# Maxima of score bounds in rounds of four banks, pieces of x through one bank, in a cross-attention kernel

## The chip, the cores and the metric

The kernel runs on one core of a Trainium2 chip. The time is the device time of one execution in microseconds (us), from the profiler's records of the core. A core has a matrix engine (TensorE, PE; its weight loads are listed apart, as PEld), a vector engine (VectorE, DVE), a scalar engine (ScalarE, ACT), GpSimd (POOL, hardly used here) and SyncE (SP), which here only issues DMAs. PE writes its results into PSUM, eight banks of 128 partitions x 512 floats, and DVE and ACT read them out.

## The reference

For each of four batches (x: 2048 rows of 640; context: 154 rows of 384, of which 150 are keys and 4 are extra tokens) it computes an ordinary attention of 8 heads over the 150 keys, and a second branch in which the four extra tokens make 384 query rows that attend over all 2048 rows of x, and whose result is projected and attends over four keys. Both are added, projected and added to x.

```python
query = hidden_states @ Wq
keyt, valt = enc @ Wk, enc @ Wv
hs = _mha(query, keyt, valt)                       # 8 heads, 150 keys
ca_q1 = jnp.einsum('btc,th->bch', ca, Wq_ca)       # 384 rows from 4 tokens
ca_q1 = ca_q1[:, indices, :]                       # rows repeated to 2048
ca_hs1 = _mha(ca_q1, residual, residual)           # attends over x itself
ca_q2 = ca_hs1 @ Wq
ca_hs2 = _mha(ca_q2, ca @ Wk_ca, ca @ Wv_ca)       # 4 keys
out = (hs + ca_hs2) @ Wout + b_out + residual
```

The softmax over 2048 rows needs, for each of the 384 rows and each head, the maximum of the scores. The kernel finds these maxima ahead of the exponentials, and that work is what the change concerns.

## The kernel before

Each batch runs through a sequence of stages, one after the other on every engine in an order written out by hand; the engines are tied together by semaphores. The stages of a batch are: keys and values; the *stage of products*; a stage of scores, exponentials and weighted sums of the second branch (`scores`, `weigh`); and sixteen tiles of 128 rows of the ordinary attention with the output projection. All batches do the same.

The stage of products works on x in four chunks (`i`) of 512 rows and five column tiles (`kt`) of 128, twenty *pieces*, numbered m = 5 i + kt; the text writes x0 to x19. For each piece PE transposes four squares into a PSUM bank (`turn_x`), ACT copies the bank to SBUF (`copy_x`, semaphore `xt_copied`), and PE multiplies the copy with a small matrix (`products`, four matmuls of 56 or 84 columns, listed as eight), which adds up over the five pieces of a chunk in two banks of `ps_w`. ACT then copies these sums to `y_all` (for chunk 0 DVE does one of the two banks), DVE splits a part of them into `gst` (`split_g`), PE transposes that into a piece bank (`turn_g`), and ACT copies it into `g` (`copy_g`, semaphore `g_ready`). Pieces of x and of g take their bank in turn: `piece_free` makes PE wait until the piece that used the bank has been copied.

A *unit of maxima* is one matmul of 12 or 28 rows by 512 columns (`max_unit`) for one chunk q, one third `ct` of the 384 rows and one of four groups `r`, which is a group of 32 rows of the array, and one read by DVE that takes the maximum over the 512 columns (`unit_maxima`, semaphore `max_free`). There are two phases of 48 units; phase 0 and twelve units of phase 1 (`UNITS_EARLY`) stand in the stage of products, in which `UNIT_ORDER` lists them, and `PHASE0_UNITS` is 60. The other 36 lie in the next stage. In the stage of products they go in triples (`TRIPLES` says behind which piece and which of three places), in the three banks of `ps_s`, which the matmuls of a triple fill next to each other in different row groups. A unit waits until the unit that had its bank before has been read. The first unit of a chunk waits for that chunk's g.

Between all that PE does matmuls of 128 x 512 for the first queries (`queries0`, 75 in a batch: five outputs j of 15 each), whose number behind each piece is `Q0_FILL`, ahead of the round and the products at the pieces in `Q0_ENDS`, behind them elsewhere; `Q0_SPLIT`, `Q0_TURNED` and `Q0_TRIPLE` are the numbers around the last g and between the last rounds. The first query of an output waits until DVE has taken the output before it from its bank. Behind the last round follow the remaining queries and `turn_ca(0)`, the three transposes of the maxima, on which the next stage rests.

What PE issues for one piece m is in this order: transposes of x(m); queries if m is in `Q0_ENDS`; triple at AFTER_TURNED; products(m - 1), with `turn_g` at every fifth; triple at AFTER_PRODUCTS; queries; triple at AFTER_QUERIES. DVE takes a chunk's twelve first units, then the split of the next g, then the chunk's other units, then the low part of the queries (`q0_lows`).

## Time and profile before

| | us |
|---|---|
| median of 3 timed runs | 1541.65 |
| lowest and highest | 1541.1, 1544.61 |
| the profiled execution's own time | 1540.79 |
| its span, first to last instruction | 1539.0 |
| TensorE busy in it | 1499.8 (97%) |
| VectorE busy | 791.1 (51%) |
| ScalarE busy | 620.0 (40%) |

The granted TensorE clock was 0.996 of full speed in the mean. Times in the rows are in microseconds from the span's start, unless marked ns. A matmul's row gives its full latency, and following ones overlap with it, so that the distance of starts is what an instruction costs PE. The line number of a matmul is that of a helper: L508 is any matmul, L518 any transpose; what tells them apart is the tile on the left of the arrow and the operands on its right. `ps_s<-ot,ca_mat` is a unit of maxima (`g` lies in the tile `ot`), `ps_w<-gyw_b,work` products, `ps_w<-xt_h,wq_h` and its like a query, `ps_t<-ident,xc` a piece of x, `ps_t<-ident,gst` a piece of g, `ps_s<-ident,cst` the transposes of the maxima.

### The profile page before, as it was taken

What the parts mean: (1) busy time and instruction counts of PE and PEld (TensorE: products, weight loads), DVE (VectorE), ACT (ScalarE), POOL (GpSimd) and SP (SyncE); (2) the same over time, 40 slices, a digit from 0 to 9 for tenths busy, and PEclk for the clock granted to TensorE, in tenths of its full rate; (3) what the DMA queues carried; (4) which work ended last, traced back from release to release, by engine and by line L of the source; (5) the groups of instructions that cost most, each with busy time, mean ns of one, the idle gap of its engine ahead of it and who ended that gap; (6) DMA issues with size and microseconds to landing.
All of it is one profiled execution on the core that took longest, in us unless ns stands there. A gap on an engine that the chain in (4) does not pass through costs nothing.

```text
span 1539.0 us, 24550 instructions
## 1 busy us (share of the span) xinstructions
PE 1499.8 (97%) x10306; PEld 1247.5 (81%) x10306; DVE 791.1 (51%) x1595; ACT 620.0 (40%) x1310; POOL 2.8 (0%) x12
## 2 busy tenths in 40 slices
PE   6999999999999999999999999999999999999998
PEld 4764699999976489999987549999998745999998
DVE  5686445344468453443447826335345882443533
ACT  1428723233243862332333584233333368333322
POOL 0000000000000000000000000000000000000000
PEclk9999999999999999999999999999999999999999
DMA  6530011130253001131035200204004510021101
GB/s 241 205 136 35 3 54 70 55 114 26 89 170 130 1 16 48 66 111 54 35 111 182 88 1 20 82 28 156 18 35 155 180 38 1 20 95 57 61 18 43
DMA packets 46680, 117.28 MB, mean 76 GB/s; under 512 B 3661, under 2 KB 5317, under 8 KB 45019
## 3 DMA queue, kind: packets, MB, share of 16 engines
q1 hardware_dynamic: 37036, 93.91, 17.4%
q10 hardware_dynamic: 9535, 21.80, 3.7%
q8 instruction: 82, 1.34, 0.3%
q14 instruction: 27, 0.22, 0.0%
HBM read 77.33 MB, written 39.17 MB: 76 GB/s over the span
## 4 chain that ended last, share of the span: by engine, by line
PE 91%; DVE 4%; ACT 2%; issue 2%; DMA 0%; SPq 0%
PE ps_w L508 46%; PE ps_s L508 19%; PE ps_t L508 16%; PE ps_t L518 5%; PE ps_w L518 3%; DVE unit_max L1311 2%; ACT work L1124 1%; PE ps_s L518 1%; ACT ot L1038 0%; DMA y_all<-in_L_xattn_Wv_ca_dram 0%; DVE ca_mat L1327 0%; DVE ot L1423 0%; ACT ot L1107 0%; DVE xt_l L1337 0%; ACT work L1021 0%
## 5 line engine op out<-in xcount | busy, mean ns | idle before, releaser
L508 PE MATMUL ps_w<-wo_h,ot 128*128 128x320 f32 x1280 | 310.4, 314 | 0.6 <-DVE ot L1423 0.6
L1311 DVE TENSOR_REDUCE unit_max<-ps_s 128x1 f32<-128x512 f32 x384 | 240.6, 683 | 53.1 <-PE ps_s L508 52.2
L1094 ACT ACTIVATE work<-ps_s,neg_max 128x150 f32<-128x150 f32 x512 | 152.5, 403 | 223.4 <-DVE neg_max L1369 223.4
L508 PEld LDWEIGHTS ps_w<-wo_h,ot 128*128 128x128 f32 x1280 | 220.3, 188 | 0.9 <-DVE ot L1423 0.9
L508 PE MATMUL ps_w<-wo_l,ot 128*128 128x320 f32 x640 | 197.4, 308 | 0.0
L508 PEld LDWEIGHTS ps_w<-v_all,work 120*128 120x128 f32 x1280 | 170.3, 190 | 3.0 <-issue 2.5
L508 PE MATMUL ps_w<-v_all,work 120*128 120x162 f32 (+1 forms) x1280 | 171.3, 288 | 0.0
L1365 DVE TENSOR_REDUCE neg_max<-ps_s 128x6 f32<-128x900 f32 x64 | 70.1, 1095 | 165.2 <-PE ps_s L508 165.2
L508 PE MATMUL ps_s<-keys_h,qt_h 128*128 128x300 f32 (+1 forms) x448 | 140.0, 313 | 0.0
L508 PE MATMUL ps_s<-keys_h,qt_l 128*128 128x300 f32 (+1 forms) x448 | 131.5, 294 | 0.0
L508 PE MATMUL ps_s<-keys_l,qt_h 128*128 128x300 f32 (+1 forms) x448 | 131.1, 293 | 0.0
L1434 DVE TENSOR_TENSOR work<-ps_w,xc 128x320 f32<-128x320 f32 x128 | 62.4, 488 | 130.9 <-PE ps_w L508 130.9
L1391 DVE TENSOR_TENSOR qt_l<-ps_t,qt_h 128x512 fp32r<-128x512 f32 x60 | 41.5, 691 | 162.1 <-ACT qt_h L1076 162.1
L508 PEld LDWEIGHTS ps_w<-wo_l,ot 128*128 128x128 f32 x640 | 120.4, 188 | 0.2
L508 PE MATMUL ps_t<-xt_h,wq_h 128*128 128x512 f32 x300 | 119.3, 398 | 0.4
L1124 ACT ACTIVATE work<-ps_w 128x768 f32<-128x768 f32 x128 | 104.2, 814 | 35.2 <-PE ps_t L508 20.8
L508 PE MATMUL ps_t<-xt_h,wq_l 128*128 128x512 f32 x300 | 117.7, 392 | 0.0
L508 PE MATMUL ps_t<-xt_l,wq_h 128*128 128x512 f32 x300 | 116.6, 389 | 0.0
L1107 ACT ACTIVATE ot<-ps_w 128x640 fp32r<-128x640 f32 x64 | 45.0, 704 | 175.1 <-PE ps_w L518 175.1
L508 PE MATMUL ps_w<-work,y_all 128*32 128x384 f32 x1024 | 109.1, 498 | 0.1
L508 PEld LDWEIGHTS ps_s<-keys_h,qt_h 128*128 128x128 f32 x448 | 84.9, 189 | 25.5 <-issue 25.0
L1076 ACT ACTIVATE qt_h<-ps_t 128x512 fp32r<-128x512 f32 x60 | 35.9, 598 | 169.3 <-PE ps_t L508 169.3
(163 smaller groups left out, 2346.9 us busy)
## 6 DMA issues: line engine op xcount, KB each, us to landing
xc<-in_x_dram SPq DMA_DIRECT2D x32, 1280.0 KB, 6.5
out_dram<-work ACTq DMA_DIRECT2D x64, 320.0 KB, 2.2
xt_all<-work SPq DMA_DIRECT2D x60, 256.0 KB, 2.2
xt_l<-xt_all SPq DMA_DIRECT2D x12, 1280.0 KB, 5.6
y_all<-in_L_xattn_Wk_dram SPq DMA_DIRECT2D x4, 960.0 KB
y_all<-in_L_xattn_Wv_dram SPq DMA_DIRECT2D x4, 960.0 KB
pick<-pick_all SPq DMA_DIRECT2D x16, 194.0 KB
xc<-in_L_xattn_Wq_dram SPq DMA_DIRECT2D x1, 1600.0 KB, 10.5
```

Source lines behind the costliest of these rows:

```text
L508: return nc.tensor.matmul(out, lhs, rhs, start=start, stop=stop, skip_group_check=True)
L518: return nc.tensor.transpose(out, in_, ident[0:k, 0:k])
L1076: nc.scalar.activation(dst, ps_t[:, bank_of(use), :], copy).then_inc(t_high, 1)
L1094: return nc.scalar.activation(probs[:, h * KEYS:(h + 1) * KEYS], ps_s[:, bank, c * KEYS:(c + 1) * KEYS], exp, bias=neg_max[:, s % 2, h:h + ...
L1107: nc.scalar.activation(ot_h[:, s % 2, :], ot_psum, copy).then_inc(ot_high, 1)
L1124: nc.scalar.activation(e_buf[n % E_BUFS][:, 2 * p:2 * p + 2, :], score_banks[p], exp, scale=SCALE).then_inc(w_ready, 1)
L1311: v.tensor_reduce(unit_max[:, a, n, q:q + 1], bank, AX_X, ALU.max).then_inc(max_free, 1)
L1365: v.tensor_reduce(neg_max[:, s % 2, 0:6].rearrange("p (a h) -> p a h", a=2), ps_s[:, 0:2, 0:3 * KEYS].rearrange("p a (h k) -> p a h k", h= ...
L1391: v.tensor_tensor(dst, ps_t[:, bank_of(use), :], high_part, ALU.subtract).then_inc(t_free[bank_of(use)], 1)
L1434: v.tensor_tensor(o_tile[:, s % 2, cols], out_banks[half], xc[:, c % 2 * ST + t, cols], ALU.add).then_inc((ya_ready, y_ready)[half], 1)
```

## The change

Units of the stage of products go in rounds of four (`G_BANKS`), one in each row group, in the three banks of `ps_s` and in bank 1 of `ps_t`. Behind them three banks are used as before. `UNIT_BANK` and `UNIT_PREVIOUS` say which bank a unit has and which unit had it before. Pieces of x and of g all take bank 0 of `ps_t`; `piece_free` waits for the copy of the piece just ahead, where it waited for the one before that. Chunk 0 has eight early units of phase 1 and chunk 1 four (six and six before), so that each chunk is made of whole rounds. `TRIPLES` becomes `ROUNDS`, at most one round at a piece, and there is none at piece 16; `Q0_FILL` and `Q0_ENDS` have other numbers, and all remaining queries stand behind the last round, ahead of `turn_ca`.

```diff
--- before.py
+++ after.py
@@ -121,12 +121,12 @@
 SW = GYW + 1
 PHASES, GROUPS = 2, 4
 UNITS = CHUNKS * CT * GROUPS
-M_BANKS = 3
+M_BANKS, G_BANKS = 3, 4
 T_BANK = 2
 E_BUFS = 2
 
 
-UNITS_EARLY = 6
+UNITS_EARLY = [8, 4, 0, 0]
 
 
 def unit_order():
@@ -135,7 +135,7 @@
     for q in range(CHUNKS):
         units = [(ct, r) for ct in range(CT) for r in range(GROUPS)]
         early += [(0, q, ct, r) for ct, r in units]
-        n = UNITS_EARLY if q + 2 < CHUNKS else 0
+        n = UNITS_EARLY[q]
         early += [(1, q, ct, r) for ct, r in units[:n]]
         late += [(1, q, ct, r) for ct, r in units[n:]]
     return early + late, len(early)
@@ -143,14 +143,15 @@
 
 UNIT_ORDER, PHASE0_UNITS = unit_order()
 AFTER_TURNED, AFTER_PRODUCTS, AFTER_QUERIES = range(3)
-TRIPLES = {8: (AFTER_TURNED, AFTER_QUERIES), 9: (AFTER_PRODUCTS,), 10: (AFTER_TURNED,), 11: (AFTER_TURNED,), 12: (AFTER_TURNED,),
-           13: (AFTER_TURNED, AFTER_QUERIES), 14: (AFTER_PRODUCTS,), 15: (AFTER_TURNED,), 16: (AFTER_TURNED,), 17: (AFTER_TURNED,),
-           18: (AFTER_TURNED, AFTER_QUERIES), 19: (AFTER_PRODUCTS,), 20: (AFTER_TURNED,)}
+ROUNDS = {8: AFTER_TURNED, 9: AFTER_TURNED, 10: AFTER_TURNED, 11: AFTER_TURNED, 12: AFTER_PRODUCTS, 13: AFTER_TURNED,
+          14: AFTER_TURNED, 15: AFTER_TURNED, 17: AFTER_PRODUCTS, 18: AFTER_TURNED, 19: AFTER_TURNED, 20: AFTER_TURNED}
+UNIT_BANK = [u % (G_BANKS if u < PHASE0_UNITS else M_BANKS) for u in range(PHASES * UNITS)]
+UNIT_PREVIOUS = [max((w for w in range(u) if UNIT_BANK[w] == UNIT_BANK[u]), default=None) for u in range(PHASES * UNITS)]
 UNITS_BEFORE_SPLIT = 12
 Y_SHARED = (0,)
-Q0_FILL = [0] * 6 + [3, 0, 4, 3, 2, 1, 2, 4, 4, 2, 2, 3, 4, 4, 1]
-Q0_ENDS = (6, 12, 17)
-Q0_SPLIT, Q0_TURNED, Q0_TRIPLE = 9, 3, 5
+Q0_FILL = [0] * 7 + [4, 3, 2, 2, 2, 2, 4, 3, 2, 3, 3, 4, 3, 2]
+Q0_ENDS = (12, 17)
+Q0_SPLIT, Q0_TURNED, Q0_ROUND = 9, 3, 5
 UNITS_STEP = [3, 2, 3, 2, 3, 2, 2, 3, 2, 3, 2, 3, 2, 2, 0, 0]
 UNREAD = 4
 UNREAD_SUMS = 3
@@ -387,7 +388,8 @@
             return before(b, use) + 1
 
 
-        piece_bank = {piece: ps_t[:, n % 2, :] for n, piece in enumerate(PIECES)}
+        piece_bank = ps_t[:, 0, :]
+        unit_banks = [ps_s[:, 0, :], ps_s[:, 1, :], ps_s[:, 2, :], ps_t[:, 1, :]]
         score_banks = [ps_w[:, 0:2, 0:CAD], ps_t[:, 0:2, 0:CAD]]
         q0_banks = [ps_w[:, 2, :], ps_w[:, 2, :], ps_w[:, 2, :], ps_w[:, 0, :], ps_w[:, 2, :]]
         sums = ps_w[:, 2, 0:CAD]
@@ -410,7 +412,7 @@
 
         def unit(u):
 
-            return (*UNIT_ORDER[u], ps_s[:, u % M_BANKS, :])
+            return (*UNIT_ORDER[u], unit_banks[UNIT_BANK[u]])
 
         @block.sync
         def _(sp):
@@ -606,7 +608,7 @@
                         pe.wait_ge(ca_base_ready, PHASES * (b + 1))
                     if n == V_ORDER[-1]:
                         pe.wait_ge(xc_in[0], 16 * (b * XC_LOADS + 1))
-                        turn_x(0, 0, piece_bank[("x", 0)], gx_turned)
+                        turn_x(0, 0, piece_bank, gx_turned)
                     at, lo, hi = KR * n % KEYS, V_HEADS[n][0] * DH, (V_HEADS[n][-1] + 1) * DH
                     for c in range(CT):
                         last = mm(v_psum(n), enc_t[:, c, at:at + KR], wv[:, c, :].rearrange("p (r n) -> p r n", r=2)[:, :, lo:hi],
@@ -635,8 +637,8 @@
                 def piece_free(piece):
 
                     n = PIECES.index(piece)
-                    if n >= 2:
-                        kind, old = PIECES[n - 2]
+                    if n:
+                        kind, old = PIECES[n - 1]
                         if kind == "x":
                             pe.wait_ge(xt_copied, b * GX + old + 1)
                         else:
@@ -647,14 +649,14 @@
                     pe.wait_ge(g_split, b * CHUNKS + i + 1)
                     piece_free(("g", i))
                     for t in range(ST):
-                        last = turned(piece_bank[("g", i)][:, t * P:(t + 1) * P], gst[:, t, :, :].rearrange("p h k -> p (h k)"))
+                        last = turned(piece_bank[:, t * P:(t + 1) * P], gst[:, t, :, :].rearrange("p h k -> p (h k)"))
                     last.then_inc(gt_full, 1)
 
                 def max_unit(u):
 
                     phase, q, ct, r, bank = unit(u)
-                    if u >= M_BANKS:
-                        pe.wait_ge(max_free, b * PHASES * UNITS + u - M_BANKS + 1)
+                    if u >= G_BANKS:
+                        pe.wait_ge(max_free, b * PHASES * UNITS + UNIT_PREVIOUS[u] + 1)
                     else:
                         pe.wait_ge(keys_ready, b + 1)
                     if phase == 0 and ct == 0 and r == 0:
@@ -695,37 +697,37 @@
                         if m == 1:
                             pe.wait_ge(vals_ready, VT_HALF * b + 2)
                         piece_free(("x", m))
-                        turn_x(i % 2, kt, piece_bank[("x", m)], gx_turned)
-
-                    def triple(place):
+                        turn_x(i % 2, kt, piece_bank, gx_turned)
+
+                    def a_round(place):
                         nonlocal first
-                        if place in TRIPLES.get(m, ()):
-                            max_units(first, M_BANKS)
-                            first += M_BANKS
+                        if ROUNDS.get(m) == place:
+                            max_units(first, G_BANKS)
+                            first += G_BANKS
 
                     if m in Q0_ENDS:
                         queries0(done, Q0_FILL[m])
-                    triple(AFTER_TURNED)
+                    a_round(AFTER_TURNED)
                     if m >= 1:
                         i, kt = divmod(m - 1, KT)
                         products(i, kt)
                         if i and kt == 1:
                             turn_g(i - 1)
-                    triple(AFTER_PRODUCTS)
+                    a_round(AFTER_PRODUCTS)
                     if m not in Q0_ENDS:
                         queries0(done, Q0_FILL[m])
                     done += Q0_FILL[m]
-                    triple(AFTER_QUERIES)
+                    a_round(AFTER_QUERIES)
                 queries0(done, Q0_SPLIT)
                 turn_g(CHUNKS - 1)
                 done += Q0_SPLIT
                 queries0(done, Q0_TURNED)
                 done += Q0_TURNED
-                for u in range(first, PHASE0_UNITS, M_BANKS):
-                    max_units(u, M_BANKS)
-                    if u + M_BANKS < PHASE0_UNITS:
-                        queries0(done, Q0_TRIPLE)
-                        done += Q0_TRIPLE
+                for u in range(first, PHASE0_UNITS, G_BANKS):
+                    max_units(u, G_BANKS)
+                    if u + G_BANKS < PHASE0_UNITS:
+                        queries0(done, Q0_ROUND)
+                        done += Q0_ROUND
 
                 def turn_ca(a):
 
@@ -897,9 +899,8 @@
                         mm(out_banks[half], p2_rows[:, c % 2, t * P:(t + 1) * P], vw2_b[:, cols], False,
                            True).then_inc(y_full, 1)
 
-                queries0(done, 2 * Q0_TRIPLE)
+                queries0(done, KT * Q0_MM)
                 turn_ca(0)
-                queries0(done + 2 * Q0_TRIPLE, KT * Q0_MM)
                 max_units(PHASE0_UNITS, 2)
                 scores(0, 0)
                 for n in range(UNREAD):
@@ -1018,7 +1019,7 @@
                             act.wait_ge(xt_ready, b * CHUNKS * KT + old + 1)
                         else:
                             act.wait_ge(xt_stored[old % XT_RING], 16 * (b * XT_STORES[old % XT_RING] + XT_NTH[old]))
-                    nc.scalar.activation(xt[:, xt_slot(m), :], piece_bank[("x", m)], copy).then_inc(xt_copied, 1)
+                    nc.scalar.activation(xt[:, xt_slot(m), :], piece_bank, copy).then_inc(xt_copied, 1)
 
                 for m in range(VT_HALF - 1):
                     take_values(m)
@@ -1035,7 +1036,7 @@
                 def copy_g(i):
 
                     act.wait_ge(gt_full, b * CHUNKS + i + 1)
-                    nc.scalar.activation(g[:, i * CHUNK:(i + 1) * CHUNK], piece_bank[("g", i)], copy).then_inc(g_ready, 1)
+                    nc.scalar.activation(g[:, i * CHUNK:(i + 1) * CHUNK], piece_bank, copy).then_inc(g_ready, 1)
 
                 def q0_highs(j):
 
@@ -1338,7 +1339,7 @@
                 split_g(0)
                 first = 0
                 for i in range(1, CHUNKS):
-                    chunk = per_chunk + (UNITS_EARLY if i < CHUNKS - 1 else 0)
+                    chunk = per_chunk + UNITS_EARLY[i - 1]
                     unit_maxima(first, UNITS_BEFORE_SPLIT)
                     split_g(i)
                     if i < CHUNKS - 1:
```

The order that this makes on TensorE at three places of a batch. L510 and L520 are in the changed kernel what L508 and L518 are in the kernel before.

From x5 to the first g. Before (`ps_t<-ident,xc` are x5, x6 and x7, the products are those of pieces 4, 5 and 6):

```order
L518 MATMUL ps_t<-ident,xc 128x128 x4
L508 MATMUL ps_w<-gyw_b,work 128x56 x4
L518 MATMUL ps_t<-ident,xc 128x128 x4
L508 MATMUL ps_w<-xt_h,wq_h 128x512
L508 MATMUL ps_w<-xt_l,wq_h 128x512
L508 MATMUL ps_w<-xt_h,wq_l 128x512
L508 MATMUL ps_w<-gyw_b,work 128x56 x4
L518 MATMUL ps_t<-ident,xc 128x128 x4
L508 MATMUL ps_w<-gyw_b,work 128x84 x4
L518 MATMUL ps_t<-ident,gst 128x128 x4
```

and now, from the products of piece 4, with the first query behind the first g:

```order
L510 MATMUL ps_w<-gyw_b,work 128x56 x4
L520 MATMUL ps_t<-ident,xc 128x128 x4
L510 MATMUL ps_w<-gyw_b,work 128x56 x4
L520 MATMUL ps_t<-ident,xc 128x128 x4
L510 MATMUL ps_w<-gyw_b,work 128x84 x4
L520 MATMUL ps_t<-ident,gst 128x128 x4
L510 MATMUL ps_w<-xt_h,wq_h 128x512
```

The three queries between x6 and products(5) have gone behind the first g.

TensorE from x12 to the products of piece 12, around the second g. Before:

```order
L518 MATMUL ps_t<-ident,xc 128x128 x4
L508 MATMUL ps_w<-xt_l,wq_h 128x512
L508 MATMUL ps_w<-xt_h,wq_l 128x512
L508 MATMUL ps_s<-ot,ca_mat 128x512 x3
L508 MATMUL ps_w<-gyw_b,work 128x84 x4
L518 MATMUL ps_t<-ident,gst 128x128 x4
L518 MATMUL ps_t<-ident,xc 128x128 x4
L508 MATMUL ps_s<-ot,ca_mat 128x512 x3
L508 MATMUL ps_w<-gyw_b,work 128x56 x4
```

and now, where a round is the two rows of `ot,ca_mat`, three units and one:

```order
L520 MATMUL ps_t<-ident,xc 128x128 x4
L510 MATMUL ps_w<-xt_l,wq_h 128x512
L510 MATMUL ps_w<-xt_h,wq_l 128x512
L510 MATMUL ps_w<-gyw_b,work 128x84 x4
L520 MATMUL ps_t<-ident,gst 128x128 x4
L510 MATMUL ps_s<-ot,ca_mat 128x512 x3
L510 MATMUL ps_t<-ot,ca_mat 128x512
L520 MATMUL ps_t<-ident,xc 128x128 x4
L510 MATMUL ps_s<-ot,ca_mat 128x512 x3
L510 MATMUL ps_t<-ot,ca_mat 128x512
L510 MATMUL ps_w<-gyw_b,work 128x56 x4
```

The round that stood ahead of products(11) stands behind the second g, and only x13 is between it and the next round.

TensorE between the last two rounds of the stage. Before:

```order
L508 MATMUL ps_s<-ot,ca_mat 128x512 x3
L508 MATMUL ps_w<-xt_l,wq_h 128x512
L508 MATMUL ps_w<-xt_h,wq_l 128x512
L508 MATMUL ps_w<-xt_h,wq_h 128x512
L508 MATMUL ps_w<-xt_l,wq_h 128x512
L508 MATMUL ps_w<-xt_h,wq_l 128x512
L508 MATMUL ps_s<-ot,ca_mat 128x512 x3
L508 MATMUL ps_w<-xt_h,wq_h 128x512
```

and now:

```order
L510 MATMUL ps_s<-ot,ca_mat 128x512 x3
L510 MATMUL ps_t<-ot,ca_mat 128x512
L510 MATMUL ps_w<-xt_h,wq_l 128x512
L510 MATMUL ps_w<-xt_h,wq_h 128x512
L510 MATMUL ps_w<-xt_l,wq_h 128x512
L510 MATMUL ps_w<-xt_h,wq_l 128x512
L510 MATMUL ps_w<-xt_h,wq_h 128x512
L510 MATMUL ps_s<-ot,ca_mat 128x512 x3
L510 MATMUL ps_t<-ot,ca_mat 128x512
L510 MATMUL ps_w<-xt_l,wq_h 128x512
```

Five queries stand between them both times. Behind the last round there are nine queries before and fourteen now, ahead of the three transposes of the maxima.

## Rows read from the trace of the kernel before

**Rows 1.** The page: busy time, share of the span and instructions of each engine.

```profile
PE 1499.8 (97%) x10306; PEld 1247.5 (81%) x10306; DVE 791.1 (51%) x1595; ACT 620.0 (40%) x1310; POOL 2.8 (0%) x12
```

**Rows 2.** Stretches: length, busy time of PE, PEld, DVE, ACT, POOL; PEclk.

```profile
60.20:116.40 56.20, 54.03 (x325) 39.13 (x324) 43.81 (x81) 16.02 (x30) 0.00 (x0) 1.00 0.48 168
1180.00:1236.20 56.20, 54.02 (x335) 39.55 (x334) 42.83 (x77) 17.59 (x33) 0.00 (x0) 1.00 0.50 172
```

**Rows 3.** Waits from 60.2 to 116.4: us in total, times, longest.

```profile
PEld ps_s L508 <- DVE unit_max L1311: 6.2, 17, 0.6
...
DVE unit_max L1311 <- PE ps_s L508: 10.3, 13, 3.4
```

**Rows 4.** Timeline of PE, batch 0: start, us, instruction [idle before].

```profile
58.52 0.60 PE L518 MATMUL ps_t<-ident,xc 128*128 128x128 f32 x4
...
59.79 0.61 PE L518 MATMUL ps_t<-ident,xc 128*128 128x128 f32 x4
...
61.67 1.07 PE L508 MATMUL ps_w<-gyw_b,work 128*128 128x56 f32 x8 [0.57 <-DVE y_all L1294]
...
63.03 1.02 PE L508 MATMUL ps_w<-gyw_b,work 128*128 128x84 f32 x8
...
64.33 0.60 PE L518 MATMUL ps_t<-ident,xc 128*128 128x128 f32 x4
65.27 0.50 PE L508 MATMUL ps_s<-ot,ca_mat 12*128 12x512 f32 x3 [0.34 <-ACT ot L1038]
...
67.16 0.39 PE L508 MATMUL ps_w<-xt_h,wq_l 128*128 128x512 f32 x1
67.39 0.40 PE L508 MATMUL ps_w<-xt_h,wq_h 128*128 128x512 f32 x1
67.72 0.50 PE L508 MATMUL ps_s<-ot,ca_mat 12*128 12x512 f32 x3
68.15 0.66 PE L518 MATMUL ps_t<-ident,xc 128*128 128x128 f32 x4
...
69.59 1.09 PE L508 MATMUL ps_s<-ot,ca_mat 12*128 12x512 f32 x3
...
79.04 0.60 PE L518 MATMUL ps_t<-ident,xc 128*128 128x128 f32 x4
...
105.75 0.60 PE L518 MATMUL ps_t<-ident,gst 128*128 128x128 f32 x4
...
116.42 0.49 PE L518 MATMUL ps_s<-ident,cst 128*128 128x128 f32 x3
```

**Rows 5.** Timeline of PEld: a triple at once, a third load that waits.

```profile
65.24 0.22 PEld L508 LDWEIGHTS ps_s<-ot,ca_mat 12*128 12x128 f32 x3 [0.55 <-issue]
...
70.19 0.18 PEld L508 LDWEIGHTS ps_s<-ot,ca_mat 12*128 12x128 f32 x1 [0.41 <-DVE unit_max L1311]
```

**Rows 6.** Timeline of DVE: six reads of maxima.

```profile
68.25 3.75 DVE L1311 TENSOR_REDUCE unit_max<-ps_s 128x1 f32<-128x512 f32 x6 [0.60 <-PE ps_s L508]
```

**Rows 7.** Timeline of ACT: copy of x5, of the first g, of y.

```profile
59.15 0.60 ACT L1021 ACTIVATE work<-ps_t 128x512 f32<-128x512 f32 x1 [0.17 <-PE ps_t L518]
...
64.53 0.60 ACT L1038 ACTIVATE ot<-ps_t 128x512 fp32r<-128x512 f32 x1 [0.70 <-PE ps_t L518]
...
88.46 0.98 ACT L1033 ACTIVATE y_all<-ps_w 128x448 f32<-128x448 f32 x2 [0.86 <-PE ps_w L508]
```

**Rows 8.** Stretches, columns as in rows 2, with lower clocks.

```profile
40.00:45.00 5.00, 5.00 (x28) 5.00 (x28) 3.25 (x9) 0.00 (x0) 0.00 (x0) 0.66 0.38 92
...
848.00:854.00 6.00, 6.00 (x24) 4.53 (x23) 3.17 (x8) 1.47 (x3) 0.00 (x0) 0.72 0.74 256
```

**Rows 9.** Timeline of PE: start of batch 0; x8 and maxima, batch 2.

```profile
37.14 1.35 PE L518 MATMUL ps_s<-ident,ctx_in 128*128 128x128 f32 x6 [1.78 <-DVE ot L1252]
...
810.98 0.60 PE L518 MATMUL ps_t<-ident,xc 128*128 128x128 f32 x4
...
864.66 0.49 PE L518 MATMUL ps_s<-ident,cst 128*128 128x128 f32 x3
```


## The prediction

> **What bounds the kernel now.** I read the page's busy times first: TensorE is busy for 97% of the span [rows 1], so what counts is its work and its idle time, batch by batch. The table by stretches comes second: the stage that the diff touches lasts 56.2 us in each of the four batches, with PE busy for 54.0 and the vector engine for 43 to 44 [rows 2]; what I find in batch 0 counts four times. The list of waits in that stage comes third: 17 weight loads of maxima sat idle for 6.2 us in all until a bank's maximum had been read, and the vector engine sat idle for 10.3 us until PE had filled one [rows 3]. Neither engine is far ahead: each triple of maxima fills all three banks, so the two take turns. The timelines then give prices. I call the maxima issued together a round, and x8 the ninth piece of x (x0 is the first).
>
> **Prices.** A triple with free banks takes PE from 67.72 to 68.15, 0.43 us, and is started 0.33 after a query matmul where the next query would start after 0.24: 0.09 more. So a round costs 0.52 [rows 4]. Its three weight loads, 0.18 each, are over in 0.22, so a further row group adds 0.02 [rows 5]: a round of four costs 0.54. The vector engine's reads follow each other at 0.625 (six in 3.75) [rows 6]. The triple at 69.59 shows the wait: its third load stands until 70.19, which is 2.47 after the triple before it began at 67.72 [rows 4, 5]. One more bank makes this 2.47 + 0.625 = 3.09: the fourth matmul of a round can't start sooner after the round before it. A piece copy on ScalarE takes 0.60 and starts 0.03 behind the end of the four transposes (x5 from 58.52 for 0.60, its copy at 59.15; PE is held for 0.44 of it) [rows 4, 7]; after the copy of g, which ends at 65.13, PE goes on at 65.27 [rows 4, 7]. So with one bank, two pieces are at least 0.60 + 0.03 + 0.60 + 0.14 = 1.37 apart.
>
> **What the change removes.** Sixty maxima per batch stand ahead of the stage's end both times, so 20 rounds become 15: 20 x 0.52 = 10.4 against 15 x 0.54 = 8.1, **2.3 us per batch saved** (9.2 in all). The number of matmuls is the same. The 75 queries, 19 products and the reads stay; products behind a round (10 times both ways) keep their price.
>
> The Trainium skill ("TensorE: Matmul & The Clock Gate", the cost: per-tile semaphore tail) gives 4.7 ns per further tile and 26.3 ns per further increment, 31 ns for the fourth. By it the sum would be 0.6 us worse over the 60 rounds than with my 0.02; no row has a fourth one.
>
> **What it adds: waits.** I walked PE, ScalarE and the vector engine through both orders with these prices, each step at the later of the engine's turn and its releaser. For the kernel before the walk gives the final transposes of the maxima 116.6 against 116.42 in the trace, and 79.0 and 105.9 for x13 and the last g against 79.04 and 105.75 [rows 4], so the prices hold. The idle time of PE in it, before and after:
>
> To x8: 0.50 and 1.37. Now three queries lie between x6 and products that wait for the copies of y, and PE is still idle for 0.57 [rows 4]. The new table has none there: the wait is 1.23. Pieces x3 to x5 followed each other at 1.27 [rows 4] and now pay up to 1.37, 0.14 in all with the turning of g.
>
> x8 to x13: 1.13 and 0.90. Before: 0.39 for the copy of g ahead of the first round (the four queries now moved there hide it), 0.64 at the third round, 0.10. After: rounds stand one a piece: round 0.45, products 0.92, three queries 0.79, a piece 0.44 and 0.09 come to 2.7 where 3.09 less three starts of 0.02 are needed, so 0.36, then 0.21 and 0.33.
>
> x13 to x18: 1.03 and 2.64. This is **the largest item**. The round behind products(11) has only x13 between it and the next one. x13 itself waits for the copy of g, since it uses g's bank: 0.38. Then from round to round 0.45 + 0.38 + 0.44 + 0.05 + 0.09 = 1.41 us of PE's time stand against 3.03: a wait of 1.6. Then 0.16, 0.17, and 0.29 at products(15), which wait for the 0.98 of the copies of y [rows 7] with no round ahead of them. From x15's round to x17's the vector engine has no maximum for some 7 us and can't make up.
>
> x18 to the last g: 1.34 and 2.79. The pair again (0.38 and 1.6), 0.16, 0.61.
>
> To the end: 1.36 and 1.98. Five queries stand between the last rounds, 1.3 of the 3.0 wanted: 1.25 and 0.68. The 14 queries behind the last round instead of 9 cover the vector engine's last reads and then some.
>
> Sum of the waits: 5.4 before, 9.7 after, **+4.3**; and 0.05 for each of seven new restarts of PE (behind a wait products last 1.07 and not 1.02 [rows 4]), +0.3. Moving queries costs nothing, all are done before the stage ends both times. Net: -2.3 + 4.3 + 0.3 = **+2.3 per batch, +9.0 in four**. Nothing behind the stage takes it back: the remaining 36 maxima go through three banks as before, and the first scores wait for the same last steps.
>
> **The clock** can add to this. The profile's rows show 2.4 GHz in nearly all stretches, and drops to 1.2 behind idle time: at 37.14 PE had been idle for 1.78 us, and the 5 us from 40 have a mean of 0.66 [rows 8, 9]. In batch 2 the stretch 848 to 854 has 0.72, behind waits for banks like all others [rows 8]; there x8 (810.98) and the transposes of the maxima (864.66) are 53.68 apart [rows 9], in batch 0 52.09 (64.33 and 116.42) [rows 4]: a drop costs 1.6. The changed kernel has eight pairs of rounds with 2.0 us of waits within 3, much like the first case. Each could bring a drop, at 1.6 less what the waits behind it absorb (0.16 and 0.17): 0 to 13 us. The long gap gave a drop, the stage's shorter waits only one in four batches; I take two further ones, one for every four pairs: +2.9.
>
> The Trainium skill ("TensorEngine Tiling (Array Packing)", PSUM Bottleneck) says that tiling speeds up TensorE but not the emptying of PSUM, which can become the limit. It speaks against this change, and it is the third rival below when taken strictly; with the rows alone PE, 54.0 of 56.2 busy, is as much the limit as the reads.
>
> **Forecast.** The profiled execution took 1540.79 (its span 1539.0 and 1.8 around it), the median of the three timed runs 1541.65. I add to the median: 1541.65 + 9.0 + 2.9 = **1553.5**, 0.8% slower. Its own range is 1549 to 1559.
>
> **Rivals.**
> - *Every pair brings the clock down* (8 x 1.6): 9 + 13 = +22, 1564. Against: in the whole of before only one stretch of the stage fell.
> - *The fourth matmul isn't concurrent.* It would then cost a query's 0.235 in place of 0.02, 60 x 0.21 = +13 on top: 1566. Against: triples already take the row groups in all combinations at one price. Decides if a round with free banks lasts 0.65 and not 0.45.
> - *The vector engine sets the pace and PE never arrives late.* Then from the first round at 66.0: 15 x 3.09, three splits of 0.64 and three low parts of 0.61 are 50.1 and 0.6 for placing the maxima: 116.7 against 116.4 now, +0.3 per batch, 1543, no difference. For: it is busy for nearly 44 of the stage's 56 us already [rows 2]. Against: PE's new order has some 7 us between two rounds around x16 and 6 around the last g, where that engine runs dry.
> - *Faster: the waits at the pairs don't come.* Bank waits are 7.3 of the 9.7 per batch. At half of that the batch comes to 2.3 - 3.65 = -1.35, 1536; with none of them to -5, 1522. The mechanism would be PE and the reads overlapping within a round (it may fill a bank while the next is read) so far that the fourth is always free. It decides where rounds are 3.1 apart; the new order has 1.4 at each pair and 1.8 at the end, and a pair escapes only if a read takes under half of its 0.625.
> - *One bank for the pieces costs more than 1.37*: if ScalarE is late with each copy by its neighbour's 0.62, 19 x 0.3 x 4 = +23. Against: ScalarE is idle for over 1.5 us ahead of nearly every copy behind x6.
>
> **How the numbers follow.** Forecast (walk with 0 to 5 drops) 0.66; clock down at most places, or late copies, 0.12; fourth not concurrent 0.04; the vector engine's pace, or waits a quarter smaller than computed, 0.10; faster 0.08. The range takes in the drops and half of the no-change cases, and leaves out the rest, under two tenths: 1543 to 1564. A measurement of this kernel can tell about 0.2% (3.1 us) from no change. Slower by more: 0.82, within: 0.10, faster by more: 0.08.
>
> **What would show it.** Rounds of four with free banks: 0.45. The fourth load of the second round of each pair idle, near 1.6 us over the round's own 0.45. Maxima reads still at 0.68 each. The products after x6 idle for 1.2 in place of 0.57. x8 at about 65.5, x13 79.8, x18 95.8, last g 108.1, transposes of the maxima 118.9 in batch 0. The waits on the reads in the stage: from 6.2 to about 8 or 9 us. The mean granted clock at or below 0.996. I am wrong if the first round of a pair meets the second without a wait, if the stage ends before 117, or if the copies of single pieces are what PE mostly waits for.

## The result and the profile after

The changed kernel took 1580.4 us (median; 1578.8 to 1589.2) against 1542.7 for the kernel before: **2.6% slower**, ratio 1.0256 (95% interval 1.0215 to 1.0296). I had forecast the direction, with 1553.5 and a range up to 1564: the time lies 16 us above the range. The profiled execution has a span of 1577.7, 38.7 more than before.

The page of the changed kernel: its span, and the busy times as in [rows 1]:

```profile
span 1577.7 us, 24554 instructions
...
PE 1535.9 (97%) x10306; PEld 1275.9 (81%) x10306; DVE 788.4 (50%) x1595; ACT 620.7 (39%) x1310; POOL 2.8 (0%) x12
```

PE executes the same 10306 matmuls and is busy for 36.1 us longer; its idle time has grown by 2.6 only. That doesn't acquit the waits: a unit that waits 0.6 us for its bank begins that much later than the one ahead of it, whose matmul is listed as busy for 0.49 of this time. So the busy time holds both waits and slower instructions. The mean granted clock tells of the second; the one-line view of the core, after:

```profile
core 0: 1577.7 us, clock 0.973
```

It was 0.996. Twice the missing share is the time at 1.2 GHz: 0.004 x 2 x 1539 = 12 us before (10 of them at the start of the first batch) and 0.027 x 2 x 1577.7 = 85 us after. Stretches of batch 0 (83.50 to 114.20) and those at low clock of batches 1 to 3, columns as in rows 2:

```profile
83.50:90.30 6.80, 6.80 (x30) 4.96 (x28) 3.56 (x6) 0.68 (x2) 0.00 (x0) 0.51 0.50 149
90.30:100.60 10.30, 9.61 (x60) 6.86 (x60) 5.97 (x12) 4.47 (x8) 0.00 (x0) 0.99 0.41 153
100.60:114.20 13.60, 13.60 (x50) 10.63 (x50) 8.17 (x16) 1.58 (x3) 0.00 (x0) 0.50 0.43 141
...
469.10:472.50 3.40, 3.40 (x14) 2.63 (x13) 2.04 (x4) 0.00 (x0) 0.00 (x0) 0.54 0.00 0
486.20:489.60 3.40, 3.40 (x14) 2.91 (x15) 2.38 (x4) 0.00 (x0) 0.00 (x0) 0.53 0.00 1
827.50:830.90 3.40, 3.40 (x20) 3.40 (x19) 0.00 (x0) 0.60 (x1) 0.00 (x0) 0.54 0.76 294
848.00:858.20 10.20, 10.09 (x37) 7.72 (x36) 5.69 (x10) 0.60 (x1) 0.00 (x0) 0.51 0.37 109
868.50:882.20 13.70, 13.70 (x50) 10.50 (x51) 8.44 (x16) 1.58 (x3) 0.00 (x0) 0.51 0.46 148
1233.70:1237.10 3.40, 3.40 (x14) 2.91 (x15) 2.40 (x5) 0.00 (x0) 0.00 (x0) 0.54 0.01 2
1250.80:1264.50 13.70, 13.70 (x50) 10.53 (x51) 8.39 (x16) 1.58 (x3) 0.00 (x0) 0.51 0.46 147
```

With one more from 445.3 (shown below) these are all the low stretches of the four stages: one behind **each of the eight pairs** (3.4 to 13.7 us long, 68 in all) and two, 445.3 and 827.5, behind the wait that follows x6 (10 in all). The timeline of PE from x6 on, around x13 and the first of these stretches:

```profile
61.64 1.07 PE L510 MATMUL ps_w<-gyw_b,work 128*128 128x56 f32 x8 [1.22 <-DVE y_all L1295]
...
65.33 0.60 PE L520 MATMUL ps_t<-ident,xc 128*128 128x128 f32 x4
65.86 0.51 PE L510 MATMUL ps_s<-ot,ca_mat 12*128 12x512 f32 x3
65.87 0.49 PE L510 MATMUL ps_t<-ot,ca_mat 12*128 12x512 f32 x1
66.30 1.10 PE L510 MATMUL ps_w<-gyw_b,work 128*128 128x56 f32 x8
...
69.35 1.12 PE L510 MATMUL ps_w<-gyw_b,work 128*128 128x84 f32 x8
...
78.58 0.50 PE L510 MATMUL ps_s<-ot,ca_mat 28*128 28x512 f32 x3
78.59 0.49 PE L510 MATMUL ps_t<-ot,ca_mat 28*128 28x512 f32 x1
79.33 0.66 PE L520 MATMUL ps_t<-ident,xc 128*128 128x128 f32 x4 [0.26 <-ACT ot L1039]
79.92 1.62 PE L510 MATMUL ps_s<-ot,ca_mat 12*128 12x512 f32 x3
81.65 0.50 PE L510 MATMUL ps_t<-ot,ca_mat 12*128 12x512 f32 x1
82.07 1.10 PE L510 MATMUL ps_w<-gyw_b,work 128*128 128x56 f32 x8
...
85.97 2.00 PE L510 MATMUL ps_w<-gyw_b,work 128*128 128x84 f32 x8
...
126.08 0.49 PE L520 MATMUL ps_s<-ident,cst 128*128 128x128 f32 x3
```

Read it against the forecast. x8 is at 65.33 (forecast 65.5), the first round of four holds PE from 65.86 to 66.30 (0.44, forecast 0.45), the products behind x6 waited 1.22 (1.23). At the pair, x13 starts at 79.33 (79.8), and the fourth matmul of the second round 1.73 after the first ones (79.92 to 81.65). Up to 83 us the walk is within half a microsecond of the chip. Then the clock falls, for 6.8 us, and products of 84 columns last 2.00 in place of 1.12; behind the second pair the same for 13.6 us. The transposes of the maxima start at 126.08, not at 118.9.

The waits in the stage, which were 6.2 us on maxima reads [rows 3], are 5.8 now (3.7 and 2.1): in the low stretches PE is late itself and its rounds meet free banks.

```profile
PEld ps_s L510 <- DVE unit_max L1312: 3.7, 10, 0.7
...
PEld ps_t L510 <- DVE unit_max L1312: 2.1, 6, 0.4
```

### The profile page after: what moved, and what is told of

It is laid out like the page before. It is cut to its first block, busy times and chain, and to the rows that moved or that the text cites. A ratio compares the mean times of both kernels' runs of the same rounds, so it can differ in the third digit from the quotient of the medians.

```text
span 1577.7 us, 24554 instructions
## 1 busy us (share of the span) xinstructions
PE 1535.9 (97%) x10306; PEld 1275.9 (81%) x10306; DVE 788.4 (50%) x1595; ACT 620.7 (39%) x1310; POOL 2.8 (0%) x12
## 4 chain that ended last, share of the span: by engine, by line
PE 91%; DVE 4%; ACT 2%; issue 2%; DMA 0%; SPq 0%
PE ps_w L510 48%; PE ps_s L510 17%; PE ps_t L510 17%; PE ps_t L520 6%; PE ps_w L520 3%; DVE unit_max L1312 3%; ACT work L1125 1%; PE ps_s L520 1%; DMA y_all<-in_L_xattn_Wv_ca_dram 0%; DVE ca_mat L1328 0%; DVE ot L1424 0%; ACT ot L1108 0%; DVE xt_l L1338 0%; ACT work L1022 0%; ACT y_all L1034 0%
## 5 line engine op out<-in xcount | busy, mean ns | idle before, releaser
L510 PE MATMUL ps_w<-wo_h,ot 128*128 128x320 f32 x1280 | 310.4, 314 | 0.6 <-DVE ot L1424 0.6
L1312 DVE TENSOR_REDUCE unit_max<-ps_s 128x1 f32<-128x512 f32 x324 | 203.4, 683 | 91.3 <-PE ps_t L510 47.6
L510 PEld LDWEIGHTS ps_w<-wo_h,ot 128*128 128x128 f32 x1280 | 220.3, 188 | 0.9 <-DVE ot L1424 0.9
L510 PE MATMUL ps_w<-wo_l,ot 128*128 128x320 f32 x640 | 197.4, 308 | 0.0
L510 PEld LDWEIGHTS ps_w<-v_all,work 120*128 120x128 f32 x1280 | 170.3, 190 | 3.1 <-issue 2.6
L510 PE MATMUL ps_w<-v_all,work 120*128 120x162 f32 (+1 forms) x1280 | 171.3, 288 | 0.0
L510 PE MATMUL ps_s<-keys_h,qt_h 128*128 128x300 f32 (+1 forms) x448 | 140.0, 313 | 0.0
L510 PE MATMUL ps_s<-keys_h,qt_l 128*128 128x300 f32 (+1 forms) x448 | 131.5, 294 | 0.0
L510 PE MATMUL ps_s<-keys_l,qt_h 128*128 128x300 f32 (+1 forms) x448 | 131.1, 293 | 0.0
L510 PEld LDWEIGHTS ps_w<-wo_l,ot 128*128 128x128 f32 x640 | 120.4, 188 | 0.2
L510 PE MATMUL ps_t<-xt_h,wq_h 128*128 128x512 f32 x300 | 119.2, 397 | 0.4
L510 PE MATMUL ps_t<-xt_h,wq_l 128*128 128x512 f32 x300 | 117.7, 392 | 0.0
L510 PE MATMUL ps_t<-xt_l,wq_h 128*128 128x512 f32 x300 | 116.7, 389 | 0.0
L510 PE MATMUL ps_w<-work,y_all 128*32 128x384 f32 x1024 | 109.1, 498 | 0.1
L510 PEld LDWEIGHTS ps_w<-gyw_b,work 128*128 128x128 f32 x640 | 91.2, 218 | 21.9 <-issue 10.9
L510 PE MATMUL ps_w<-gyw_b,work 128*128 128x56 f32 (+1 forms) x640 | 99.2, 306 | 7.2 <-DVE y_all L1295 4.9
```

What stands on the lines that cost most here:

```text
L510: return nc.tensor.matmul(out, lhs, rhs, start=start, stop=stop, skip_group_check=True)
L1312: v.tensor_reduce(unit_max[:, a, n, q:q + 1], bank, AX_X, ALU.max).then_inc(max_free, 1)
```

## The experiments

**Theory A**: the waits of a pair of rounds bring the clock down, and the low clock is most of the loss. Rivals: rounds of four or the single piece bank do it by themselves (B), or the waits are the loss and the clock is a by-product (C).

**e1: work in the wait.** Five matmuls of 128 x 512, results unused.

```diff
                         piece_free(("x", m))
+                        if m in (13, 18):
+                            for n in range(5):
+                                mm(piece_bank, wq_h[:, n, 0:P], xt_h[:, n, :], True, True)
                         turn_x(i % 2, kt, piece_bank, gx_turned)
```

> The changed kernel with five matmuls of 128 x 512 added ahead of x13 and of x18 (into the piece bank, which the transposes then overwrite; 40 added matmuls in all, 5 x 0.24 = 1.2 us a place). They lie in the 1.6 us for which the second round of each pair waits. Theory A (the idle time at the pairs brings the clock down, and the low clock is most of the loss): the waits shrink to about 0.5 us, the low stretches behind the pairs are gone or nearly so, and the time is that of the walk, 1550 to 1556, although work is added. Theory B (the clock falls whatever the pairs do, from rounds of four or from the table of queries): unchanged, 1578 to 1585, clock near 0.973. Theory C (the loss is in the waits themselves, the clock only a by-product): the same as B or worse.

Measured 1561.2 (1554.4 to 1562.3), ratio 1.0109 (1.0084 to 1.0134): with 40 matmuls more, **19 us less** than the changed kernel. A's range, 1550 to 1556, is missed by 5: three of its four executions have a clock of 0.987, the profiled one is the fastest. The pair in its timeline:

```profile
81.20 1.42 PE L510 MATMUL ps_t<-xt_h,wq_h 128*128 128x512 f32 x5 [0.25 <-ACT ot L1042]
82.46 0.60 PE L520 MATMUL ps_t<-ident,xc 128*128 128x128 f32 x4
82.99 0.51 PE L510 MATMUL ps_s<-ot,ca_mat 12*128 12x512 f32 x3
83.51 0.49 PE L510 MATMUL ps_t<-ot,ca_mat 12*128 12x512 f32 x1
```

and its span and mean granted clock:

```profile
core 0: 1552.6 us, clock 0.992
```

The fourth matmul waits 0.5 now, and behind none of the eight pairs is the clock low. B and C are out as the cause of most of the loss: the order of rounds and pieces is the same.

**e7: transposes in the wait.** As e1, with twelve transposes of the piece itself in place of the five matmuls.

> As e1, but with twelve transposes of 128 x 128 (the piece's own, repeated) ahead of x13 and x18 in place of the five matmuls: 12 x 0.11 = 1.3 us of work a place. If transposes keep the clock up as matmuls do, the time is that of e1, 1554 to 1562, clock 0.99; if they do not count for it, the low stretches stay, 1575 to 1590, clock near 0.973.

Measured 1559.5, ratio 1.0113 (1.0092 to 1.0133). Transposes help as much as the large matmuls of e1: the clocks of the four executions are 0.986 to 0.991 here and 0.987 to 0.992 there. (The profiled executions, 44 us at low clock here and 25 in e1, are the slowest of this run and the fastest of e1.)

**e2: the pair taken apart.** The two rounds stand ahead of the products and of g.

```diff
-ROUNDS = {..., 12: AFTER_PRODUCTS, ..., 17: AFTER_PRODUCTS, ...}
+ROUNDS = {..., 12: AFTER_TURNED, ..., 17: AFTER_TURNED, ...}
```

> The changed kernel with only the places of the rounds at pieces 12 and 17 moved from behind the products and the turning of g to right behind the transposes (AFTER_TURNED), so that products and g lie between the two rounds. The walk: transposes of the maxima of batch 0 at 116.9 in place of 118.9, so without low clock +1.4 us in all, 1543 to 1545; x13 and x18 then wait 0.9 for g's copy. Theory A: the low stretches behind the pairs go or become few (single waits of 0.9 and 0.6 as in the kernel before, which had one): 1544 to 1552, clock 0.99 or more. Theory B: 1570 to 1580, clock still near 0.975.

Measured 1547.9 (1542.4 to 1560.3), ratio 1.0036 (1.0013 to 1.0060), clock 0.991. Two words in a table are worth 32 us, of which the walk explains 8. The runs spread over 18 us, with clocks from 0.996 down to 0.980.

**e3: triples, one piece bank.** In the kernel before, `piece_bank` is `ps_t[:, 0, :]` for every piece, and `piece_free` waits for the piece just ahead.

> The kernel before with one thing of the change alone: all pieces take bank 0 of ps_t. The walk: x8, x13 and x18 wait 0.9 for the copy of g and nothing else is added, +1.9 us per batch, 1549. Theory A: waits of 0.9 in place of 0.4 may bring a few low stretches, 1548 to 1556. If the single bank were what costs (a rival), it would come near the 1580 of the changed kernel.

Measured 1550.1, ratio 1.0051 (1.0034 to 1.0069), clock 0.997. The single bank costs the walk's 8 us and next to no clock.

**e4: triples in pairs.** In the kernel before, the triples at pieces 12 and 17 go from AFTER_TURNED to AFTER_PRODUCTS.

> The kernel before with one thing of the change's order alone: the triples at pieces 12 and 17 stand behind the products and g, so that with the next triple they make a pair like that of the changed kernel; two piece banks, three maxima banks. The walk: the second triple of a pair waits 1.5 in place of 0.4, transposes of the maxima at 118.6 in place of 116.6, +8 us in all without low clock. Theory A (pairs bring the clock down): low stretches behind the pairs, 1560 to 1580, clock 0.98 or less. Theory B (it takes four banks): 1548 to 1552, clock 0.995.

Measured 1586.5 (1574.3 to 1590.5), ratio 1.0269 (1.0222 to 1.0315): **the whole loss, with three banks, triples and two piece banks**, and 6 us above A's upper end. Timeline of PE at its second pair:

```profile
94.47 0.50 PE L508 MATMUL ps_s<-ot,ca_mat 28*128 28x512 f32 x3
94.89 0.66 PE L518 MATMUL ps_t<-ident,xc 128*128 128x128 f32 x4
95.74 1.68 PE L508 MATMUL ps_s<-ot,ca_mat 12*128 12x512 f32 x3 [0.19 <-DVE unit_max L1311]
97.35 1.95 PE L508 MATMUL ps_w<-gyw_b,work 128*128 128x56 f32 x8
```

and the stretch, columns as in rows 2:

```profile
97.00:113.50 16.50, 16.50 (x55) 12.34 (x56) 8.58 (x16) 2.02 (x4) 0.00 (x0) 0.51 0.40 131
```

PE is busy for all of these 16.5 us and the clock stays down. In the profiled execution such a stretch follows the second pair of each batch and no first pair, though the first pair waits just as long:

```profile
79.48 1.69 PE L508 MATMUL ps_s<-ot,ca_mat 12*128 12x512 f32 x3 [0.19 <-DVE unit_max L1311]
```

So the wait of a pair can bring the clock down and need not; what tells the two pairs apart was not tested.

**e5, e9, e11: how long a wait it takes.** The maxima are read over fewer columns, which shortens the waits and leaves the order alone. Such a kernel leaves out a part of each maximum: half of its columns in e5 and e9, seven eighths in e11. e9 adds e1's five matmuls to e5.

```diff
-                        v.tensor_reduce(unit_max[:, a, n, q:q + 1], bank, AX_X, ALU.max).then_inc(max_free, 1)
+                        v.tensor_reduce(unit_max[:, a, n, q:q + 1], bank[:, 0:256] if u < PHASE0_UNITS else bank, AX_X, ALU.max).then_inc(max_free, 1)
```

> The changed kernel with the reads of the 60 maxima per batch in the stage of products cut to the first 256 of 512 columns, so the maximum of half of the columns is left out; all else is the same. A read then takes about 0.36 in place of 0.625, and a round's fourth bank is free after about 2.0 us in place of 3.09. The walk: wait of the second round of a pair 0.6 in place of 1.6, transposes of the maxima at 112.8 in place of 118.9. Theory A (waits at the pairs bring the clock down): hardly any low stretch, 1541.65 - 4 x 3.8 = 1526 to 1532, clock 0.99 or more; that is 14 us less than the kernel before. If the clock fell from the rounds of four themselves: 1545 to 1560, clock below 0.985.

Measured 1539.2 (1534.8 to 1548.8), ratio 0.9990 (0.9968 to 1.0011): 41 us less than the changed kernel, but 12 above the walk. The expectation of hardly any low stretch was wrong: the clocks are 0.980 to 0.990, and in the profiled execution (0.980, one of the two slowest of ten) a low stretch follows all eight pairs. Its second round still waits at the pair, 0.66 from its first matmuls to the fourth:

```profile
81.06 0.66 PE L520 MATMUL ps_t<-ident,xc 128*128 128x128 f32 x4 [0.25 <-ACT ot L1039]
81.65 0.82 PE L510 MATMUL ps_s<-ot,ca_mat 12*128 12x512 f32 x3
82.31 0.49 PE L510 MATMUL ps_t<-ot,ca_mat 12*128 12x512 f32 x1
```

and its span and mean granted clock:

```profile
core 0: 1546.9 us, clock 0.980
```

So two explanations were open: a shorter wait is enough (A), or no wait is needed at all because the stretch has no query in it (D).

> e5 and e1 together: the reads of the 60 maxima per batch take the first 256 columns only (half of the maximum left out), and five matmuls of 128 x 512 are added ahead of x13 and x18. The walk: the waits at the pairs are 0.6, so of 1.2 us added a place some 0.6 to 0.8 are net work: +5 to +6 us against e5's walk of 1526, 1531 to 1532. Theory A in its first form (only waits bring the clock down; e5's waits of 0.4 and 0.6 were still enough): low stretches gone, 1531 to 1536. Theory D (it is the share of large matmuls around the pair, with or without waits): the same numbers, since work is added there too, but then e9 is faster than e5 although it does 9.6 us more work. If the clock is not what holds e5 up: 1544 to 1549.

Measured 1533.1, ratio 0.9929 (0.9907 to 0.9950), clock 0.993: with the added matmuls 6 us less than e5. It is the clock that holds e5 up, but A and D expect the same here.

> The changed kernel with the reads of the 60 maxima per batch cut to the first 64 of 512 columns (seven eighths of each maximum left out). A read takes about 0.2, and no round waits for a bank any more; of the waits at the pairs only the 0.38 for g's copy is left. The walk: transposes of the maxima at 111.3, 7.5 less per batch than the changed kernel, 1521. Theory A (waits bring the clock down): no low stretches, 1520 to 1526, clock 0.995. Theory D (the stretch around a pair, g's turning, two rounds, two pieces and products with no query among them, is too light even without a wait): low stretches stay, 1530 to 1545, clock below 0.99.

Measured 1521.7 (1520.4 to 1524.2), ratio 0.9872 (0.9857 to 0.9887), the walk's 1521. At the pair nothing waits but x13:

```profile
80.13 0.50 PE L510 MATMUL ps_s<-ot,ca_mat 28*128 28x512 f32 x3
80.14 0.49 PE L510 MATMUL ps_t<-ot,ca_mat 28*128 28x512 f32 x1
80.89 0.66 PE L520 MATMUL ps_t<-ident,xc 128*128 128x128 f32 x4 [0.26 <-ACT ot L1039]
81.48 0.50 PE L510 MATMUL ps_s<-ot,ca_mat 12*128 12x512 f32 x3
81.49 0.49 PE L510 MATMUL ps_t<-ot,ca_mat 12*128 12x512 f32 x1
```

and its span and mean granted clock:

```profile
core 0: 1520.9 us, clock 0.994
```

The stretch without queries does not bring the clock down as long as nothing but x13 waits: no pair has a low stretch behind it, and D alone falls.

**e12: work beside the wait.** e1's five matmuls, put behind `piece_free(("g", i))` for i in (1, 2), right before the pair.

> The changed kernel with e1's five matmuls of 128 x 512 put ahead of the second and third turning of g, so right before a pair and not in its wait: the waits stay at 0.38 and 1.6, and the added 1.2 us a place are net work, +9.6 in all. The walk with the clock up: 1541.65 + 9.1 + 9.6 = 1560. Theory A (the waits alone decide): the low stretches of the changed kernel stay, 1580.4 + 9.6 = 1590. Theory D (the share of large matmuls near the pair decides): a good part of the low stretches goes, 1565 to 1578, so less than the changed kernel although work was only added.

Measured 1576.9 (1576.1 to 1578.5), ratio 1.0231 (1.0213 to 1.0248), clock 0.982. A's 1590 is missed by 13 and D's upper end, 1578, holds: the waits are all there, and with large matmuls ahead of them there is less low time (57 us against 85). It also lies elsewhere: behind the pairs 17 us in place of 68, all behind the first pair of a batch, but 27 behind the last rounds of the stage, 6.8 in each batch, where the changed kernel waits just as long (1.24 and 0.6) and keeps its clock:

```profile
118.70 1.14 PE L510 MATMUL ps_s<-ot,ca_mat 12*128 12x512 f32 x3
119.94 0.50 PE L510 MATMUL ps_t<-ot,ca_mat 12*128 12x512 f32 x1
```

So the waits alone don't tell where the clock falls. What else does was not settled.

**Where the low stretches lie.** Read from the granted clock of the profiled executions, each with 7 to 10 us more at the start of the first batch; us at 1.2 GHz, and how often:

| | behind pairs | behind x6 | behind the last rounds |
|---|---|---|---|
| changed kernel | 68 (8 of 8) | 10 (2) | 0 |
| e1 work in the wait | 0 | 7 (1) | 7 (1) |
| e7 transposes | 0 | 14 (3) | 20 (3) |
| e2 pair apart | no pairs | 3 (1) | 14 (2) |
| e4 triples in pairs | 68 (4 of 8) | 0 | 0 |
| e5 256 columns | 41 (8 of 8) | 10 (3) | 0 |
| e9 256 columns, work | 0 | 10 (3) | 0 |
| e11 64 columns | 0 | 10 (2) | 0 |
| e12 work beside | 17 (4 of 8) | 0 | 27 (4) |

Wherever the wait of the second round is filled or gone, no pair has a low stretch behind it; where it is there, four or all of the eight have. The other two places, with waits of 1.2 each, bring one in some batches and not in others.

**e6, e8, e10: tables that keep rounds apart.** I looked for numbers of `ROUNDS`, `Q0_FILL`, `Q0_ENDS`, `Q0_SPLIT`, `Q0_ROUND` for which the walk ends early and never waits more than about a microsecond in a short time. e6 and e10 have four banks, e8 is the same for triples and two piece banks.

```diff
-ROUNDS = {8: AFTER_TURNED, 9: AFTER_TURNED, 10: AFTER_TURNED, 11: AFTER_TURNED, 12: AFTER_PRODUCTS, 13: AFTER_TURNED,
-          14: AFTER_TURNED, 15: AFTER_TURNED, 17: AFTER_PRODUCTS, 18: AFTER_TURNED, 19: AFTER_TURNED, 20: AFTER_TURNED}
+ROUNDS = {8: AFTER_TURNED, 9: AFTER_QUERIES, 10: AFTER_QUERIES, 11: AFTER_QUERIES, 12: AFTER_PRODUCTS, 13: AFTER_PRODUCTS,
+          14: AFTER_QUERIES, 15: AFTER_QUERIES, 16: AFTER_PRODUCTS, 17: AFTER_QUERIES, 19: AFTER_TURNED, 20: AFTER_QUERIES}
-Q0_FILL = [0] * 7 + [4, 3, 2, 2, 2, 2, 4, 3, 2, 3, 3, 4, 3, 2]
-Q0_ENDS = (12, 17)
-Q0_SPLIT, Q0_TURNED, Q0_ROUND = 9, 3, 5
+Q0_FILL = [0, 0, 0, 0, 0, 0, 5, 4, 0, 0, 2, 3, 1, 0, 5, 5, 5, 0, 2, 0, 1]
+Q0_ENDS = (6, 9, 12, 13, 16, 19)
+Q0_SPLIT, Q0_TURNED, Q0_ROUND = 13, 3, 7
```

> The changed kernel with other numbers in the table of rounds and queries alone: rounds about 3 us of PE's work apart, queries between each turning of g and the piece behind it, three to seven queries between the last rounds, five ahead of products(5). The walk: waits of PE from x6 on 4.6 in place of 9.6 us per batch, none over 0.8, transposes of the maxima at 112.5, that is 4.0 less than for the kernel before. Theory A: no or few low stretches, 1524 to 1532. If four banks are a loss by themselves (a rival): not below 1542.

> The kernel before (triples, two piece banks) with other numbers in its tables, found with the same walk and the same aim as those of e6. It tells how much of e6's gain is the table and how much the fourth bank. The walk: transposes of the maxima at 114.5, 2.1 less per batch than before, 1533 to 1536 with the clock up. If the fourth bank brought nothing, it would equal e6.

> A second table for four banks, found as e6's; its walk ends at the same 112.5, with the same waits in other places. It tells whether e6's 1529 belongs to the walk's number or to that one table: 1526 to 1532 if to the walk, with the clock at 0.99 or more; otherwise anything up to 1545.

e6: 1528.9 (1528.1 to 1529.6), ratio **0.9914 (0.9899 to 0.9929)**, clock 0.993. e10: 1528.6, ratio 0.9906 (0.9891 to 0.9921). e8: 1541.7, ratio 0.9998 (0.9984 to 1.0012), clock 0.990. e6 around its second g, where products and x13 lie between the rounds, and at the end of the stage:

```profile
77.67 0.50 PE L509 MATMUL ps_s<-ot,ca_mat 28*128 28x512 f32 x3
78.10 0.50 PE L509 MATMUL ps_t<-ot,ca_mat 28*128 28x512 f32 x1
78.53 0.66 PE L519 MATMUL ps_t<-ident,xc 128*128 128x128 f32 x4
79.02 1.00 PE L509 MATMUL ps_w<-gyw_b,work 128*128 128x56 f32 x8
79.95 0.69 PE L509 MATMUL ps_s<-ot,ca_mat 12*128 12x512 f32 x3
80.74 0.50 PE L509 MATMUL ps_t<-ot,ca_mat 12*128 12x512 f32 x1
...
113.02 0.55 PE L519 MATMUL ps_s<-ident,cst 128*128 128x128 f32 x3
```

Even here the closest rounds, 2.3 apart, wait 0.8 for the fourth bank, and in batches 1 and 3 the clock falls behind them. Four banks with a fitting order are 0.9% faster than before; the order of the change lost it. e8 is one table for triples, found by the same walk, and doesn't prove that none is better. e8 missed its 1533 to 1536 by some 6 us: its low time is 31 us where before had 12.

**The two terms together.** The price of low clock is taken from the changed kernel alone: span +38.7, walk +9.1, the remaining 29.6 over 85 - 12 = 73 us more at low clock, 0.41 for each. Applied to the other profiled spans (change against 1539.0; low time is twice the missing clock times the span):

| | walk x 4 | low time | sum | measured |
|---|---|---|---|---|
| e1 work in the wait | +9.1 | 25 | +14 | +13.6 |
| e2 pair apart | +1.4 | 28 | +8 | +6.5 |
| e3 one piece bank | +7.6 | 9 | +6 | +8.5 |
| e4 triples in pairs | +8.1 | 75 | +34 | +33.5 |
| e5 256 columns | -15.3 | 62 | +5 | +7.9 |
| e6 evenly | -16.2 | 21 | -13 | -11.2 |
| e7 transposes | +9.1 | 44 | +22 | +22.2 |
| e8 triples evenly | -8.3 | 31 | -1 | +0.9 |
| e10 evenly | -16.2 | 18 | -14 | -11.1 |
| e11 64 columns | -21.0 | 18 | -19 | -18.1 |
| e12 work beside | +18.5 | 57 | +37 | +36.0 |

The sum is within 3 us everywhere. e9 fits too: its recorded walk of 1531 to 1532 is -10, 21 us at low clock make it -6, and its span changed by -6.9. The price doesn't hang on the walk: among the ten executions each of e2, e5 and e8, spans and clocks on record give 0.38, 0.45 and 0.42 for a microsecond at low clock. With 0.41 all recorded executions of these kernels are within 4 us of the sum. So the walk of the waits holds, and what it lacks is the clock.

## Why the prediction was wrong

- *Rounds save 2.3 per batch*: right, a round of four with free banks holds PE for 0.44, so the fourth runs beside the others.
- *Waits cost 4.3 per batch, the pairs most*: right. The wait at the fourth matmul was 1.7 with forecast 1.6, the one behind x6 1.22 with 1.23, those between the last rounds 1.24 and 0.60 with 1.25 and 0.68. Of the 38.7 in the span the walk explains 9.1; the other 29.6 are what the price above gives for 73 us at low clock.
- *Two further drops at up to 1.6 us, +2.9*: **the step that failed**. That the waits at the pairs bring the clock down was right, e1 and e4 show it. The size was ten times too small, +29.6 for +2.9, and by two factors. The number: I took one drop for every four pairs, as the shorter waits of the stage of before had given one in four batches, but all eight pairs had one. The length: I took that of the one drop in the stage of before, 3.4 us, but behind a pair the clock stayed down for 3.4 to 13.7 us, in e4 for 17, with PE busy nearly throughout. So 7 us more at low clock were forecast and 73 came. The price of a microsecond was right: 1.6 for 3.4 is 0.47, measured 0.41. And a place that I had priced at its wait alone, the 1.2 us behind x6 among transposes and products, is followed by a low stretch in batches 1 and 2:

```profile
445.30:452.10 6.80, 6.80 (x31) 6.31 (x31) 0.39 (x2) 1.19 (x2) 0.00 (x0) 0.51 0.47 176
```

- *The range up to 1564*: it stood on the rival that every pair brings the clock down, which came true. I had given it little chance because the stage of before had one drop only, though that stage has no such pair, and had priced its eight drops at 1.6 each. With the 68 us at low clock that lie behind the pairs it comes to 1579.
- *The rival that the vector engine sets the pace* fell: e6 has the same 60 reads in 15 rounds from 66.6 on and ends its stage at 113.0, where this rival allows 117 at the earliest. *The faster rival* fell too: the waits at the pairs came, at 1.7. It took 3.1 us between rounds as what a free fourth bank needs; in e6 they start 2.3 to 5.1 apart, and it still gains. *The fourth matmul* is concurrent (a round takes 0.44), and *the single piece bank* cost in e3 what the walk said.
- Of what would show it: a mean clock at or below 0.996 was far too mild; the waits on reads did not rise to 8 or 9, since the slow PE met free banks.

## What to carry to other kernels

Cost a wait of TensorE twice: its own length, and the chance that it brings the clock down, for up to ten times the wait (here 17 us behind about 1.5, e4). One drop in the kernel at hand is no measure of how many and how long they are in another order. Where rounds share all their banks with one reader, place them about a full read-out apart (here 0.49 + 4 x 0.625) and put large matmuls between the turning of a piece and the next use of its bank (e6 does both; what each gives was not measured), and compare the mean granted clock of two orders before reading anything else. A better resource can lose in an order made for the old one; try it with an order of its own before giving it up.

## What the runs showed of the hardware that I had not expected

- Adding 40 large matmuls to a kernel bound by TensorE made it 19 us faster (e1), and 96 repeated transposes in the same places took 21 us off (e7).
- At low clock PE ran for 13.6 and 16.5 us without idle time, and the clock did not rise in these stretches of transposes, products of 56 and 84 columns, rounds and a few large matmuls.
- A wait of 0.66 for a bank behind one of 0.25 for a piece still brought low clock behind all eight pairs (e5, 62 us in the run); the latter alone did so behind none (e11, 18 us in the run, 7 at the start of the first batch and 10 behind the wait of 1.2 that follows x6).
- The same wait of 1.7 us was followed by 17 us at low clock at one place of a batch and by none at another (e4).
- A microsecond at 1.2 GHz cost 0.41 us here, not 0.5. Queries start 0.43 apart there (102.89 to 103.31 in the changed kernel) and 0.235 at 2.4 GHz, so that a microsecond still does the work of 0.55; where the rest goes was not measured.
